# A two-block transformer kernel on one core: Silu as one ScalarE operation, norm constants on VectorE, input loads on SP, and a new hand-written order

## What is computed

```python
cmod = silu(c) @ w_ada + b_ada            # shift, scale, gate, twice: 6 x 128 per sequence
x_mod = ln(x) * (1 + scale_msa) + shift_msa
k, q, v = split(x_mod @ w_qkv)            # softmax(q k^T / 8) v, 16 heads
x = x + gate_msa * (attention @ w_proj + b_proj)
x = x + gate_mlp * (gelu((ln(x) * (1 + scale_mlp) + shift_mlp) @ w_mlp1 + b) @ w_mlp2 + b)
```

## Time and profile before

| | us |
|---|---|
| median of 3 runs (lowest, highest) | 95.74 (95.59, 96.35) |
| the profiled execution, device time | 95.43 |
| its span, first to last instruction | 93.6 |
| PE busy (share of the span) | 82.8 (88%) |
| DVE busy | 73.7 (79%) |
| POOL busy | 63.3 (68%) |
| ACT busy | 63.1 (67%) |
| chain that ended last | PE 57%, DVE 26%, issue 7%, POOL 5%, ACT 1% |

### The profile page before, as it was taken

How to read it: one execution, slowest core, us unless ns; L and a number is a source line. 1 busy time by engine, 2 the same in 40 slices (tenths; PEclk the granted TensorE clock), 3 DMA queues, 4 the chain that set the end, 5 groups by cost and what they waited for, 6 DMA issues and landing times.

```text
span 93.6 us, 4637 instructions
## 1 busy us (share of the span) xinstructions
PE 82.8 (88%) x1904; PEld 57.5 (61%) x1904; DVE 73.7 (79%) x209; ACT 63.1 (67%) x129; POOL 63.3 (68%) x117
## 2 busy tenths in 40 slices
PE   3998999977985998899998999999999999997920
PEld 3996646735653685558564676558476775776810
DVE  2598798999999879994089998746399748969990
ACT  0707999966892387338970669999954547899720
POOL 6967489995599129999655199049807399895400
PEclk9999999999999999999999999999999999999999
DMA  1939994000000000000000000000000000000033
GB/s 37 304 148 308 419 399 196 0 10 3 7 0 7 0 0 3 7 0 0 0 7 0 0 7 0 7 0 7 0 7 3 7 0 7 7 3 7 7 112 112
DMA packets 2532, 5.04 MB, mean 54 GB/s; under 512 B 336, under 2 KB 1872, under 8 KB 2256
## 3 DMA queue, kind: packets, MB, share of 16 engines
q1 hardware_dynamic: 2080, 4.23, 12.5%
q10 hardware_dynamic: 432, 0.52, 1.6%
HBM read 4.23 MB, written 0.52 MB: 51 GB/s over the span
## 4 chain that ended last, share of the span: by engine, by line
PE 57%; DVE 26%; issue 7%; POOL 5%; ACT 1%; DVEq 0%; POOLq 0%; ACTq 0%
PE ps_p L640 8%; PE ps_p L645 7%; PE ps_s L699 7%; PE ps_p L711 7%; DVE rden_T L1004 6%; POOL Kb L550 4%; DVE neg_max L982 4%; PE ps_s L570 4%; PE ps_p L736 3%; PE ps_p L584 3%; DVE E L993 3%; PE ps_p L665 2%; PE ps_p L570 2%; DVE tok L1021 2%; PE ps_p L654 2%
## 5 line engine op out<-in xcount | busy, mean ns | idle before, releaser
L824 ACT ACTIVATE PT<-ps_p 128x512 f32<-128x512 f32 x24 | 14.0, 598 | 5.4 <-PE ps_p L711 5.1
L535 POOL TENSOR_TENSOR E<-E,neg_max 128x320 f32<-128x320 f32 x16 | 11.5, 726 | 8.6 <-DVE neg_max L977 8.6
L711 PE MATMUL ps_p<-ident,E 128*128 128x128 f32 x96 | 14.6, 278 | 0.3 <-issue 0.3
L550 POOL TENSOR_SCALAR Kb<-k_raw,cols,head_mask 128x240 f32<-128x240 f32 (+1 forms) x24 | 12.1, 518 | 3.8 <-ACT k_raw L779 3.8
L711 PEld LDWEIGHTS ps_p<-ident,E 128*128 128x128 f32 x96 | 10.9, 141 | 2.8 <-issue 1.5
L816 ACT ACTIVATE Vz<-V_turned 20x384 f32<-20x384 f32 (+1 forms) x24 | 11.5, 483 | 0.8 <-DVE V_turned L902 0.2
L766 ACT ACTIVATE hidden<-ps_p,cols 128x384 f32<-128x384 f32 (+1 forms) x12 | 6.1, 544 | 6.5 <-PE ps_p L640 6.3
L640 PE MATMUL ps_p<-xm,w_rest_sb 128*128 128x384 f32 (+1 forms) x24 | 8.7, 470 | 1.0 <-DVE xm L893 0.9
L969 DVE TENSOR_TENSOR E<-ps_s,bias_dir 128x320 f32<-128x320 f32 x16 | 7.7, 479 | 1.8 <-PE ps_s L699 1.8
L819 ACT ACTIVATE Vz<-V_turned,quad_mask 128x256 f32<-128x256 f32 (+2 forms) x16 | 7.8, 522 | 0.0
L736 PEld LDWEIGHTS ps_p<-Vz,PT 128*32 128x32 f32 x512 | 5.7, 111 | 3.2 <-issue 1.5
(11 more groups left out here) (100 smaller groups left out, 189.5 us busy)
## 6 DMA issues: line engine op xcount, KB each, us to landing
tok<-in_adj SPq DMA_DIRECT2D x1, 1408.0 KB, 5.6
w_rest_sb<-in_w_rest SPq DMA_DIRECT2D x1, 1088.0 KB, 7.9
xT<-in_xT SPq DMA_DIRECT2D x1, 512.0 KB, 8.7
x_tok<-in_x_tok ACTq DMA_DIRECT2D x1, 320.0 KB, 3.9
w_ada_sb<-in_w_ada SPq DMA_DIRECT2D x1, 256.0 KB, 4.0
out<-x_tok SPq DMA_DIRECT2D x1, 256.0 KB, 2.7
w_qkv_sb<-in_w_qkv SPq DMA_DIRECT2D x1, 192.0 KB, 3.5
out<-x_tok SPq DMA_DIRECT2D x1, 192.0 KB, 2.1
```

The costliest lines, as they stand in the source:

```text
L535: pool.tensor_tensor(e, e, neg_max[:, i % 3, :].unsqueeze(2).broadcast_to([P, H, M]), ALU.add)\
L550: ins = pool.tensor_scalar(Kb1[d][:, batches(h), q, :], k_raw[:, d, 0:n, :], cols[:, R_K + d:R_K + d + 1], head_mask[:, q:q + 1], ALU.add, ...
L711: ins = pe.transpose(ps[:, j * P:(j + 1) * P], E[:, i % 3, j * HI:(j + 1) * HI, :], ident[:, :])
L824: act.activation(PT[:, i % PT_RING, :, :], psum_of(("turn", i))[:, :].rearrange("p (j t) -> p j t", t=P), ACT.Exp)\
```

## The change

Silu becomes one ACT activation straight from cols, with a one-element Exp behind it; the three silu operations of DVE fall away, and DVE's stage keeps only the two additions of 1 (renamed `scales`). The epsilon and the negated mean move from POOL to DVE, as tensor-tensor operations with two new constant tiles, and stand ahead of the semaphore that POOL waits for. ACT issues only the first load of x; the other two go to SP, one before and one after w_qkv, ahead of the rest of w_ada. `WARM` goes from 7 to 6, the fills from five stages (7 products) to three (8 products), and `ORDER` and `BANKS` are new throughout; the set of all other stages is the same. Cut to its core:

```diff
-WARM = 7
+WARM = 6
 ORDER = [
-    ("zero", ("pad",)), ("masks", 0), ("zero", ("values", 1, 0)), ("stats", (0, 0)), ("silu", 0), ("stats", (0, 1)),
-    ("dense", ("cmod", 0)), ("biases", 0), ("rstd", (0, 0)), ("rstd", (0, 1)), ("apply", 0),
-    ("fill", (3, "dense", ("xnT", 0))), ("dense", ("xnT", 0)), ("apply", 1), ("take", (("cmod", 0), 0)),
...
-    ("rstd", (0, 3)), ("scores", 0), ("apply", 3), ("take", (("v", 1), 0)), ("spread", (0, 1, 0, 2)),
...
-    ("dense", ("x1tok", 0)), ("max", 4), ("turn", 3), ("label", 3), ("stats", (1, 0)), ("label", 4),
-    ("rstd", (1, 0)), ("values", 2), ("spread", (0, 2, 0, 0)), ("spread", (0, 3, 0, 3)), ("exp", 3),
...
-    ("dense", ("xn2T", 1)), ("exp", 5), ("take", (("xn2T", 1), 0)), ("exp", 6), ("values", 5), ("recip", 5),
-    ("take", (("xn2T", 1), 1)), ("values", 6), ("recip", 6), ("mult", 5), ("dense", ("rowsum", 0)), ("mult", 6),
+    ("masks", 0), ("stats", (0, 0)), ("rstd", (0, 0)), ("scales", 0), ("apply", 0), ("dense", ("cmod", 0)),
+    ("dense", ("xnT", 0)), ("stats", (0, 1)), ("take", (("cmod", 0), 0)), ("rstd", (0, 1)),
+    ("take", (("xnT", 0), 0)), ("apply", 1), ("zero", ("ones", 0)), ("zero", ("pad",)), ("take", (("xnT", 0), 1)),
+    ("fill", (5, "dense", ("k", 0))), ("dense", ("k", 0)), ("dense", ("q", 0)), ("stats", (0, 2)),
+    ("dense", ("v", 0)), ("take", (("q", 0), 0)), ("take", (("k", 0), 0)), ("take", (("v", 0), 0)),
+    ("dense", ("xnT", 1)), ("rstd", (0, 2)), ("take", (("k", 0), 2)), ("take", (("xnT", 1), 0)),
+    ("take", (("k", 0), 1)), ("take", (("k", 0), 3)), ("take", (("xnT", 1), 1)), ("stats", (0, 3)),
+    ("fill", (2, "scores", 0)), ("scores", 0), ("max", 0), ("zero", ("values", 1, 1)), ("dense", ("k", 1)),
+    ("rstd", (0, 3)), ("spread", (0, 0, 0, 2)), ("spread", (0, 0, 0, 3)), ("apply", 2), ("dense", ("q", 1)),
+    ("take", (("q", 1), 0)), ("dense", ("xnT", 2)), ("take", (("xnT", 2), 0)), ("spread", (0, 0, 0, 1)),
+    ("take", (("k", 1), 0)), ("take", (("k", 1), 3)), ("sub", 0), ("dense", ("cmod", 1)), ("label", 0),
+    ("take", (("k", 1), 2)), ("take", (("k", 1), 1)), ("dense", ("v", 1)), ("take", (("xnT", 2), 1)),
+    ("fill", (1, "scores", 1)), ("scores", 1), ("apply", 3), ("take", (("v", 1), 0)), ("take", (("cmod", 1), 0)),
...
+    ("scores", 4), ("max", 4), ("dense", "qz"), ("dense", ("x1tok", 0)), ("stats", (1, 0)), ("label", 3),
+    ("label", 4), ("label", 5), ("label", 6), ("exp", 2), ("rstd", (1, 0)), ("sub", 4), ("spread", (0, 2, 0, 3)),
...
+    ("take", (("mlp2", 0), 0)), ("values", 5), ("label", 9), ("take", (("mlp2", 0), 1)), ("take", (("xn2T", 1), 0)),
+    ("dense", ("rowsum", 0)), ("take", (("xn2T", 1), 1)), ("exp", 6), ("take", (("rowsum", 0), 0)),
+    ("dense", ("self", 0)), ("recip", 5), ("dense", ("mlp1", 1, 3)), ("dense", ("mlp1", 1, 2)),
...
             sp.dma_start(w_ada_sb[:, 0:j * P], w_ada[:, 0:j * P]).then_inc(ld["ada0"], 16)
-            sp.dma_start(w_qkv_sb[:, :], w_qkv).then_inc(ld["qkv"], 16)
+            for n, (g0, g1) in enumerate(X_LOADS):
+                if n == 2:
+                    sp.dma_start(w_qkv_sb[:, :], w_qkv).then_inc(ld["qkv"], 16)
+                if n:
+                    sp.dma_start(x_tok[:, g0:g1, :], x_dram[:, g0:g1, :]).then_inc(ld_x[n], 16)
             sp.dma_start(w_ada_sb[:, j * P:6 * P], w_ada[:, j * P:6 * P]).then_inc(ld["ada1"], 16)
...
                 pool.wait_ge(var_ready, nth("stats", (layer, c)))
-                by_scalar = layer == 0 and APPLY_ON[c] == "ACT"
-                pool.tensor_scalar(var_eps[:, layer, g0:g1], meanvar[:, g0:g1, 1], 1.0, LN_EPS, ALU.mult, ALU.add)\
-                    .then_inc(pool_own, 1)
-                if by_scalar:
-                    pool.tensor_scalar(neg_mean[:, g0:g1], meanvar[:, g0:g1, 0], -1.0, 0.0, ALU.mult, ALU.add)\
-                        .then_inc(pool_own, 1)
-                own_n += 1 + by_scalar
-                pool.wait_ge(pool_own, own_n)
                 ins = pool.tensor_tensor(rstd[:, layer, g0:g1], var_eps[:, layer, g0:g1], minus_half[:, 0:g1 - g0],
                                          ALU.pow)
...
+            pool.memset(eps[:, :], LN_EPS).then_inc(eps_ready, 1)
+            pool.memset(minus_one[:, :], -1.0).then_inc(eps_ready, 1)
...
-            for n, (g0, g1) in enumerate(X_LOADS):
-                act.dma_start(x_tok[:, g0:g1, :], x_dram[:, g0:g1, :]).then_inc(ld_x[n], 16)
+            g0, g1 = X_LOADS[0]
+            act.dma_start(x_tok[:, g0:g1, :], x_dram[:, g0:g1, :]).then_inc(ld_x[0], 16)
             act.wait_ge(ld["cols"], 16)
-            act.activation(silu_t[:, 0, :], cols[:, R_COND:R_COND + B], ACT.Exp, scale=-1.0).then_inc(silu_e, 1)
+            act.activation(silu_c[:, :], cols[:, R_COND:R_COND + B], ACT.Silu).then_inc(silu_ready, 1)
+
+            act.activation(exp_first[:, :], cols[:, 0:1], ACT.Exp, scale=0.0)
...
                     ins = dve.bn_aggr(meanvar[:, g, :], stats[:, g, :])
-                return ins
+                wait_own(ins)
+                dve.wait_ge(eps_ready, 2)
+                if by_scalar:
+                    dve.tensor_tensor(neg_mean[:, g0:g1], meanvar[:, g0:g1, 0], minus_one[:, 0:g1 - g0], ALU.mult)
+                return dve.tensor_tensor(var_eps[:, layer, g0:g1], meanvar[:, g0:g1, 1], eps[:, 0:g1 - g0], ALU.add)
...
-            def silu():
+            def scales():
                 dve.wait_ge(consts_ready, 1)
-                dve.wait_ge(silu_e, 1)
-                wait_own(dve.tensor_tensor(silu_t[:, 1, :], silu_t[:, 0, :], ones[:, 0:B], ALU.add))
-                wait_own(dve.reciprocal(silu_t[:, 0, :], silu_t[:, 1, :]))
-                dve.tensor_tensor(silu_c[:, :], silu_t[:, 0, :], cols[:, R_COND:R_COND + B], ALU.mult)\
-                   .then_inc(silu_ready, 1)
+                dve.wait_ge(ld["cols"], 16)
```

212 lines of the change are left out of this document (103 added, 109 removed), and 9 rows, old and new, of the table BANKS.

## The result

| kernel | median us (lowest to highest) | executions | profiled execution, us | its span |
|---|---|---|---|---|
| before | 95.98 (95.44 to 98.27) | 20 | 95.43 | 93.6 |
| changed | 95.38 (94.53 to 96.65) | 20 | 95.49 | 93.7 |

The ratio is 0.993, 95% interval 0.9912 to 0.9949; in two further sets of runs, each with the kernel before beside it, it was 0.9911 (0.9876 to 0.9945) and 0.9914 (0.988 to 0.9947). So the change is worth 0.6 to 0.9 us. I had forecast 94.4, a gain of 1.3 us. The direction held and the outer range (93.2 to 96.9) held; the forecast's own range (93.4 to 94.9) did not. The size is about half, and inside the 1% that I had set as the bound for "no difference".

The account below looks back on a forecast made before the run. VectorE, with ScalarE just behind, bounds to about 30 us, then PE. Gains 1.1 + 0.4 less 0.3 make 1.2, rounded to 1.3: span 92.3, plus 1.83 outside and 0.3 for the median: 94.4. Own range 93.4 to 94.9, outer 93.2 to 96.9.

Parts of the forecast that it names:

- Silu, table loads, memset, loads of x: At the start: silu_c at about 3.1 for 4.56, second table load hidden, norm applied from 4.4, x loads hidden.
- The five fills (10 passes) end by then: TensorE's filling passes ahead of chunk 0's keys end by 6.7, so k starts at 6.7 for 7.35.
- max 1 at 13.0: VectorE's max 1, behind scores 1 at 12.35, comes at 13.0 for 14.70: 1.7 earlier.
- Adding DVE's operations one behind the other ... mult 4 ending at 28.9: VectorE's stretch to mult 4, summed with the old overlaps, ends at 28.9 for 30.0: 1.1 earlier.
- xT and w_rest, behind it, are wanted near 20 only: Loads at the start: xT and w_rest are issued behind w_ada and not needed until near 20 us.
- The 0.78 stall: mlp1 of piece 1 stood 0.78 behind xm; doing recip 5 after it removes the stall, counted as 0.4.
- There the lead stays if nothing new stalls: In PE's stretch, behind the first 30 us, the lead is kept; distances between maker and user about as before.
- the lead is given back: Rival, 25%: two or three new waits of the size of 0.78 in PE's stretch eat 1.3; time 95.7.
- The price of shared operands: VectorE's new operations with two SBUF inputs contend with a reading POOL: 0 to 1.7, taken as 0.3.
- The label chain: Rival, 15%: POOL's labels, ending at 24.5 with 0.1 us of slack, delay DVE; 97.4 at 3 later.
- The base of the sum, 93.6: Profiled span of the kernel before, from which 1.3 was taken; 0.3 was added for the median over that run.

Follow-up runs that it names:

- order_alone: The kernel before with the new order, banks and WARM, but the old operations and loads: ratio 0.9955 to the kernel before.
- x_on_act: The changed kernel with all three loads of x issued by ScalarE: ratio 0.9896 to the kernel before, four executions.
- xt_late: The changed kernel, but SP waits for the first values group before it issues the load of xT: ratio 0.9895 to the kernel before.
- after_again: The changed kernel run once more, unedited, on another chip: ratio 0.9911 to the kernel before.
- after_third: The changed kernel once more, unedited, beside two others on one chip: ratio 0.9914 to the kernel before, 95.22 us.
- spreads_later: The changed kernel with three ScalarE spreads, which serve unit 15 and later, moved behind the exponential of unit 13: ratio 0.9889 to the kernel before.
- dve_spreads: The changed kernel with three spreads of unit 2 copied by VectorE instead of ScalarE, at the same places: ratio 0.9871 to the kernel before.
- all_three: The changed kernel with xT's load held, three spreads moved later and two copied by VectorE: ratio 0.9812 to the kernel before, 94.62 us.
- few_fills: The changed kernel with two filling passes ahead of the first key product in place of five: ratio 0.9961 to the kernel before.
- old_order: The changed kernel's operations and SP's loads under the order, banks and WARM of the kernel before: ratio 1.0124 to the kernel before.

## Why the prediction was half right

*Silu, table loads, memset, loads of x: right.* These took the times forecast: silu_c 2.92 (3.1 forecast), table hidden, apply 4.48 (4.4), xm 6.64 (6.53), norm of chunk 1 at 6.87 (6.8), scores 0 at 9.03 (8.9), adj's issue 7.25 (7.1), label 0 at 12.93 (12.9).

*"The five fills (10 passes) end by then": wrong by 0.4.* They ran at 0.229 each to 7.2, so k 0 started at 7.15 and not 6.7. I had their time from before, where these passes take 0.125. TensorE starts at half pace (the 14 warm passes of before take 0.24 each), and the moment at which the pace doubles differs between executions, from about 4.5 to 7.4 and in `order_alone` and `x_on_act` near 10; `xt_late` had the ten over in 1.22 and k 0 at 6.78. The clock column prints 1.00 in the slow stretch as in the fast one, so "granted in full throughout" in the profile before was read too simply.

*max 1 at 13.0: 13.53.* The late k 0 is not the cause: in `xt_late` it starts 0.37 earlier and max 1 0.05. My sum had scores 1 right behind ScalarE's copies (forecast to end at 12.05, measured 11.97). It stands behind two filling passes of its own, and these behind VectorE's sub 0, which frees the only bank for scores (forecast 12.2, measured 12.37):

```profile
12.42 0.30 PEld L570 LDWEIGHTS ps_s<-ident 128*128 128x128 f32 x2 [0.63 <-DVE E L996]
...
12.84 0.23 PEld L699 LDWEIGHTS ps_s<-Kb,q0T 32*32 32x32 f32 x32
```

*"Adding DVE's operations one behind the other ... mult 4 ending at 28.9": the step that failed.* It ended at 30.12. The sum let VectorE run without a wait from 4.4 to 29, and asked of each load only whether its data were in time: "xT and w_rest, behind it, are wanted near 20 only". That TensorE would be stopped while they are in flight was in no term. The 1.1 of the sum measured -0.1 in the profiled pair. With xT held (`xt_late`) max 3 is 0.83 before that of the kernel before and mult 4 ends at 29.64, 0.4 early: so the pause is about 0.5 of the 1.2 by which this term was over. Of the rest, 0.4 in `xt_late` is one var_eps (below); what else takes the lead between max 1 and mult 4 was not traced and stays open.

*The 0.78 stall: the mechanism right, the size too small.* I took 0.4. The stall is gone, and from mult 4 (0.1 late) to 38.46 (1.0 early) the changed kernel gains 1.1.

*"There the lead stays if nothing new stalls": wrong, and the likeliest rival ("the lead is given back") is what happened, but not as I told it.* I looked for two or three new waits of an order made badly. It was one engine, ScalarE, with 11 us of unbroken work between 57 and 68, which the windows of before showed at 8.75 of 10 beside a PE at 10.00. I read PE-bound from that and did not ask how far ScalarE was behind. And part of what is given back is none of the order's doing: the stops in the tail, told above.

*The price of shared operands, 0.3: not met, by luck.* The seven var_eps took 153 to 164 ns and the three neg_mean 160 to 161, but nine of these ten ran with POOL idle or in a memset alone, and the tenth only beside the end of an operation that reads SBUF (quad_mask, L500). In `xt_late`, where VectorE is earlier, one did meet the labels (label_bias, POOL, 24.10 to 24.82):

```profile
24.29 0.55 DVE L849 TENSOR_TENSOR var_eps<-meanvar,eps 128x2 f32<-128x2 f32 x1
```

It took 548 ns for 160, so the mechanism and the bound of 0.56 stand. The rule of the Trainium skill (SBUF — State Buffer, Who interferes with whom) also shows in an operation that stands in both kernels: relu (L1028) takes 282 ns at the least and 859 at 78.95, where POOL's subtraction runs from 78.94 to 79.66. In before its longest was 358, but there two of the eight ysum were long, 839 and 559. Over both groups VectorE spends 0.7 us more in the changed kernel. In `after_again` that relu took 416, in `after_third` 865, and the ratios are 0.9911 and 0.9914, so little of it reaches the end.

*The label chain: right, and just so.* The labels end at 24.48; rstd of piece 0 waits for VectorE's var_eps at 25.16 and not the other way. With the load held the two come together (24.82 and 24.84).

*Against one execution.* The base of the sum, 93.6, was a good execution of before. I added 0.3 for the median over it; on the 20 executions it is 0.55.

Of the 1.3 forecast, then, about 0.4 us is given up at 17.4 with the load in flight and 0.2 to 0.6 in ScalarE's stretch, measured by what the edits that took them away gave back at the end (`spreads_later` 0.9889 and `dve_spreads` 0.9871, for 0.9911 to 0.993). Put back together (`all_three`), they give 1.5 us (medians) to 1.8 us (ratio) off the kernel before. That this is near my 1.3 is no merit of the forecast, which had neither of the two losses in it.

## What to carry to other kernels

A lead of one engine is worth what the next shared place lets through: before adding it to the end, walk it to each stretch in which a second engine is over 85% busy, and look there for work that isn't owed yet. Put such work later, or give it to an engine that has time; here both seem to have paid, by 0.2 to 0.6%. And a start made faster runs into the loads still in flight; hold back a load that is wanted late, and expect nothing of it in a kernel that isn't early. When an engine stops inside a group of like instructions, count its instructions up to the stop in several programs before looking at the data.

## What the runs showed of the hardware

- TensorE can stand in the middle of a group of like products, where the profile shows nothing that it waits for: 1.03 us after 2 of 32 in five traces, 0.76 in a sixth, and 0 to 0.48 with a load of 512 KB held back. In nine traces of different programs the stop is behind 212 weight loads and ends 2.3 to 2.5 us after the start of a 16 KB packet of kind "instruction". Shorter ones of this kind, 0.3 to 0.9 us, come in the tail (74.96 above).
- TensorE's first products run at half pace (a warm pass 0.24 us, a filling pass later 0.125), and the pace doubles at 4.5 to 7.4 us, in two traces near 10; the clock column prints 1.00 in both stretches.
- An idle TensorE of 1.2 us at the start was followed by granted clocks of 0.51 and 0.63 in the windows from 8 to 12 in one execution of `few_fills`, and one of 1.12 by 0.50 from 9 to 12 in one of `old_order`. By the mean granted clocks, most other executions of the two kernels had no such fall, and their times were alike.
- No time was lost behind a table load: 2.93 + 1.28 = 4.21, and the small Exp starts at 4.23. Both tables, Silu's and Exp's, took 1.28.
- A VectorE operation of 128 x 2 elements with both inputs in SBUF took 548 ns beside a POOL operation on two SBUF tiles, and 153 to 164 with POOL idle or in a memset.
- A copy of 20 x 384 floats took 500 to 901 ns on VectorE and 520 on ScalarE.
